# Four quads of gathered rows on chip instead of two, and attention's operands under the expert buffers

## The reference

```python
x = x + attention(layernorm(x))        # 16 heads of 128, causal; W_K, W_Q, W_V, W_O
x = x + ffn(layernorm(x))
# ffn: 32 experts, 8 of them for each token, besides a shared expert of width 256
topk_idx, topk_w = route(x)            # sigmoid scores, 4 of 8 groups kept, top 8, weights normed, times 2.5
coeff = zeros(T, E).at[arange(T)[:, None], topk_idx].add(topk_w)
for g, u, d, c in experts:             # gate, up, down: 256 to 128 and back
    out += c[:, None] * ((silu(x @ g.T) * (x @ u.T)) @ d.T)
out += silu(x @ shared_gate.T) * (x @ shared_up.T) @ shared_down.T
```

## Time and profile before

| | |
|---|---|
| median of 3 runs | 1460.2 us (1456.81 to 1460.44) |
| the profiled execution | 1459.2 us |
| its span | 1457.5 us |
| TensorE busy | 1327.4 us (91%), mean granted clock 0.973 |
| DVE busy | 961.8 us (66%) |
| ScalarE busy | 723.9 us (50%) |
| POOL busy | 610.6 us (42%) |
| DMA | 218.55 MB, mean 150 GB/s |

### The profile page before, as it was taken

How to read it: one execution, slowest core, us unless ns; L and a number is a source line. 1 busy time by engine, 2 the same in 40 slices (tenths; PEclk the granted TensorE clock), 3 DMA queues, 4 the chain that set the end, 5 groups by cost and what they waited for, 6 DMA issues and landing times.

```text
span 1457.5 us, 29253 instructions
## 1 busy us (share of the span) xinstructions
PE 1327.4 (91%) x8754; PEld 1167.5 (80%) x8754; DVE 961.8 (66%) x2024; ACT 723.9 (50%) x1664; POOL 610.6 (42%) x571
## 2 busy tenths in 40 slices
PE   5999999999999898998999999999888888789883
PEld 4888888888888786887778888888678878779883
DVE  5666667666678777687866766666686533356538
ACT  2555555555555444444455555555355545445441
POOL 4634536426342722303064553630005654445556
PEclk9999999999999899999999999999999999899997
DMA  3355443463452440000021111110459998999963
GB/s 121 113 170 180 135 139 130 151 209 112 139 170 70 166 153 15 19 12 26 5 66 37 65 39 55 43 61 30 142 198 382 341 363 260 362 387 326 334 186 90
DMA packets 120184, 218.55 MB, mean 150 GB/s; under 512 B 9504, under 2 KB 91424, under 8 KB 120096
## 3 DMA queue, kind: packets, MB, share of 16 engines
q1 hardware_dynamic: 56688, 132.58, 26.4%
q10 hardware_dynamic: 51120, 51.26, 10.5%
q0 software_dynamic: 12288, 33.57, 6.7%
HBM read 121.42 MB, written 95.94 MB: 149 GB/s over the span
## 4 chain that ended last, share of the span: by engine, by line
PE 63%; DVE 12%; DMA 11%; issue 6%; ACT 3%; POOL 2%; SPq 1%; another core or an unknown queue 1%; ACTq 0%; DVEq 0%; POOLq 0%
PE ps_t L795 6%; PE ps_s L735 6%; PE ps_s L737 6%; PE ps_s L736 6%; PE ps_x L735 5%; PE ps_x L736 5%; PE ps_x L737 5%; DMA xq<-xs 4%; PE ps_z L735 4%; PE ps_z L737 4%; PE ps_z L736 4%; DMA ring<-ws 4%; PE ps_t L735 3%; PE ps_t L737 2%; PE ps_t L736 2%
## 5 line engine op out<-in xcount | busy, mean ns | idle before, releaser
L1055 ACT ACTIVATE prob<-ps_s,neg_max 128x128 f32<-128x128 f32 (+7 forms) x256 | 189.6, 742 | 299.9 <-DVE neg_max L1236 289.2
L1251 DVE TENSOR_TENSOR pT_lo<-ps_t,pT_hi 128x512 fp32r<-128x512 f32 (+2 forms) x320 | 191.2, 601 | 66.0 <-ACT pT_hi L1071 57.9
L1236 DVE TENSOR_REDUCE neg_max<-ps_s 128x1 f32<-128x128 f32 (+7 forms) x256 | 188.7, 749 | 11.3 <-PE ps_s L786 9.8
L795 PE MATMUL ps_t<-ident,prob 128*128 128x128 f32 x1152 | 180.7, 275 | 15.4 <-DVE pT_lo L1251 9.4
L633 POOL DMA_INDIRECT xs<-xn,slots x128 | 127.0, 993 | 156.6 <-PE ps_z L737 108.2
L1071 ACT ACTIVATE pT_hi<-ps_t 128x512 fp32r<-128x512 f32 (+2 forms) x320 | 165.0, 534 | 50.9 <-PE ps_t L795 47.6
L795 PEld LDWEIGHTS ps_t<-ident,prob 128*128 128x128 f32 x1152 | 140.9, 141 | 49.8 <-DVE pT_lo L1251 15.6
L560 POOL TENSOR_TENSOR a_hi<-raw_a,zero 128x512 fp32r<-128x512 f32 x32 | 33.4, 1043 | 284.2 <-PE ps_x L737 258.3
L735 PE MATMUL ps_s<-k_hi,q_hi 128*128 128x512 f32 (+2 forms) x384 | 148.6, 387 | 0.7 <-DVE k_lo L1231 0.4
L736 PE MATMUL ps_s<-k_lo,q_hi 128*128 128x512 f32 (+2 forms) x384 | 133.5, 348 | 0.0
L737 PE MATMUL ps_s<-k_hi,q_lo 128*128 128x512 f32 (+2 forms) x384 | 133.4, 347 | 0.0
(11 more groups left out here) (288 smaller groups left out, 3882.6 us busy)
## 6 DMA issues: line engine op xcount, KB each, us to landing
ring<-ws SPq DMA_DIRECT2D x60, 768.0 KB
ws<-split_to SPq DMA_DIRECT2D x34, 768.0 KB, 4.1
xs<-taken SPq DMA_DIRECT2D x16, 1536.0 KB, 10.1
xq<-xs ACTq DMA_DIRECT2D x48, 512.0 KB
xs<-yq ACTq DMA_DIRECT2D x48, 512.0 KB
raw<-experts_dram SPq DMA_DIRECT2D x34, 384.0 KB, 4.6
raw_a<-w_a_dram SPq DMA_DIRECT2D x15, 512.0 KB, 10.4
raw_o<-w_o_dram SPq DMA_DIRECT2D x31, 128.0 KB
```

The costliest lines, as they stand in the source:

```text
L795: last = pe.transpose(bank[:, j * P:(j + 1) * P], prob[c][:, j, n * P:(n + 1) * P], ident[:, :])
L1055: act.activation(prob[c][:, j, 0:width(r)], ps_s[r % 2][:, 0:width(r)], ACT.Exp, bias=neg_max[:, r:r + 1], accum_out=row_sum[:, c, j:j + 1 ...
L1236: dve.tensor_reduce(neg_max[:, r:r + 1], ps_s[r % 2][:, 0:width(r)], AX.X, ALU.max, negate=True).then_inc(s_max, 1)
L1251: dve.tensor_tensor(lo, ps_t[m % 2][:, j * P:], hi.bitcast(F32), ALU.subtract).then_inc(s_bank_free, 1)
```

## The change

Four quads of rows are on chip instead of two (XQ). The first four are issued behind A(0), and quad q+4 when quad q is evicted. Batch 1's quads can be loaded only when its scatter is done; so its first quad (24) is issued where it was before, at the second task of quad 22, and its quads 25 and 26 with it; the two places before that issue nothing (rows_due). The memory comes from moving nine of attention's operands into the region that it releases. Ten gather buffers that lay in them are gone and eight new ones are added, so GATHERS is 62. The number of transfers, their sizes and all computation stay.

```diff
--- before.py
+++ after.py
@@ -100,7 +100,7 @@
-YQ, GATHERS = 4, 64
+YQ, XQ, GATHERS = 4, 4, 62
@@ -279,12 +279,7 @@
     raw_a, a_hi, a_lo = sb("raw_a", [P, 1024]), sb("a_hi", [P, 1024], F32R), sb("a_lo", [P, 1024], F32R)
-    raw_b, b_hi, b_lo = sb("raw_b", [P, 512]), sb("b_hi", [P, 512], F32R), sb("b_lo", [P, 512], F32R)
-    raw_o = sb("raw_o", [P, 2, D])
-    o_hi = [sb(f"o_hi{a}", [P, D], F32R) for a in range(2)]
-    o_lo = [sb(f"o_lo{a}", [P, D], F32R) for a in range(2)]
-    pL_hi, pL_lo = sb("pL_hi", [P, 2 * P], F32R), sb("pL_lo", [P, 2 * P], F32R)
-    z_hi, z_lo = sb("z_hi", [P, NQ], F32R), sb("z_lo", [P, NQ], F32R)
+    raw_b = sb("raw_b", [P, 512])
@@ -326,6 +321,12 @@
+        b_hi, b_lo = [sb(w, [P, 512], F32R, attention) for w in ("b_hi", "b_lo")]
+        raw_o = sb("raw_o", [P, 2, D], F32, attention)
+        o_hi = [sb(f"o_hi{a}", [P, D], F32R, attention) for a in range(2)]
+        o_lo = [sb(f"o_lo{a}", [P, D], F32R, attention) for a in range(2)]
+        pL_hi, pL_lo = [sb(w, [P, 2 * P], F32R, attention) for w in ("pL_hi", "pL_lo")]
+        z_hi, z_lo = [sb(w, [P, NQ], F32R, attention) for w in ("z_hi", "z_lo")]
@@ -340,14 +341,12 @@
-    yg = [sb(f"yg{n}", [P, D])[:, :] for n in range(16)]
+    yg = [sb(f"yg{n}", [P, D])[:, :] for n in range(24)]
...
-    yg += [t[:, n * D:(n + 1) * D].bitcast(F32) for t in (b_hi, b_lo) for n in range(2)]
-    yg += [t[:, :].bitcast(F32) for t in (*o_hi, *o_lo)] + [raw_o[:, a, :] for a in range(2)]
-    xq = [sb(f"xq{n}", [P, 4, D])[:, :, :] for n in range(2)]
+    xq = [sb(f"xq{n}", [P, 4, D])[:, :, :] for n in range(XQ)]
@@ -922,12 +921,12 @@
-                pe.wait_ge(s_xq[u // 2 % 2], 16 * (u // 4) + 16)
+                pe.wait_ge(s_xq[u // 2 % XQ], 16 * (u // 2 // XQ) + 16)
@@ -1079,8 +1078,15 @@
-            act.dma_start(xq[q % 2], xs[b][i * NQ:(i + 1) * NQ, :].rearrange("(t p) d -> p t d", p=P))\
-                .then_inc(s_xq[q % 2], 16)
+            act.dma_start(xq[q % XQ], xs[b][i * NQ:(i + 1) * NQ, :].rearrange("(t p) d -> p t d", p=P))\
+                .then_inc(s_xq[q % XQ], 16)
+
+        def rows_due(u):
+
+            q = u // 2 + XQ
+            if u % 2 == 0 or q >= B * PT // 2 or PT // 2 <= q < PT // 2 + XQ - 2:
+                return []
+            return range(PT // 2, q + 1) if q == PT // 2 + XQ - 2 else [q]
@@ -1099,7 +1105,7 @@
-                    for q in range(2):
+                    for q in range(XQ):
                         load_rows(q)
@@ -1119,8 +1125,8 @@
-                if u % 2 and u // 2 + 2 < B * PT // 2:
-                    load_rows(u // 2 + 2)
+                for q in rows_due(u):
+                    load_rows(q)
```

More of the change, by code:

```diff
@@ L396, in build @@
     s_ring, s_w = [sem(f"ring{n}") for n in range(RING)], sem("weights")
-    s_xq, s_xT, s_xs_hi, s_xs_lo = [sem(f"xq{n}") for n in range(2)], sem("xT"), sem("xs_hi"), sem("xs_lo")
+    s_xq, s_xT, s_xs_hi, s_xs_lo = [sem(f"xq{n}") for n in range(XQ)], sem("xT"), sem("xs_hi"), sem("xs_lo")
     s_gu, s_silu, s_h = sem("gu"), sem("silu"), sem("h")
@@ L929, in transpose_rows @@
                     last = pe.transpose(ps_xT[u % 2][:, at:at + P],
-                                        xq[u // 2 % 2][:, u % 2 * 2 + j, d * P:(d + 1) * P], ident[:, :])
+                                        xq[u // 2 % XQ][:, u % 2 * 2 + j, d * P:(d + 1) * P], ident[:, :])
             last.then_inc(s_xT, 1)
```

## The result

The changed kernel takes 1448.1 us (median of 6 runs, 1446.3 to 1451.0), the kernel before 1458.5 (6 runs, 1453.4 to 1463.2): a ratio of 0.9926, interval 0.9899 to 0.9954. It is 10.4 us faster. The profiled execution took 1448.1 us, its span is 1446.3, 11.2 us less than before.

The account below looks back on a forecast made before the run. TensorE, busy 91% of the span, was held in the expert part by late row loads while DMA engines were full. Terms 15 + 1 + 2 - 1 = 17 us gave 1443 us, range 1429 to 1458.

Parts of the forecast that it names:

- What bounds, and the lead: Expert part: row loads take 11.9 us against 8.3 us of lead; four quads give 19.4, removing 22.7 us of waits.
- Memory: Moved attention operands and 62 gather buffers instead of 64: no cost, at most 1 us for the last two gathers.
- More loads at once: Extra row loads at task 0 and before batch 1, 0.374 us per issue on ScalarE: cost 1 us, 0 to 1.5.
- Stretches up to 1240: Expert part before batch 1's weights: gains of 2 us (1130 to 1178) and 1 us (1178 to 1210, bound by weights).
- Stretch 1240 to 1385: Batch 1's full-DMA stretch: gain 15 us, from 3 to 21; limits 20.8 (TensorE) and 15.2 to 27 (DMA).
- the 7 us for the clock: 1240 to 1385: TensorE's granted clock of 0.90 and 0.91 loses at most 13.9 us; half taken as gain, 7 us.
- the 13.8 us of waits: 1240 to 1385: TensorE's waits for rows, 10.6 + 3.2 us, all taken as possible gain.
- DMA-bound throughout (1455): Rival, chance 0.25: every wait for rows becomes a wait for weights; only early bytes gain, 5.4 us less 1.
- Everything goes (1425): Rival, chance 0.10: the weight ring's lead absorbs all; 22.7 us of waits and some 12 us of half clock go.
- slower (1479): Rival, chance 0.06: the row backlog delays 36 weight loads; 1 us longer each costs 18 us, 2 us gives 1479.
- nothing (1460): Rival, chance 0.04: another wait, hT_lo at 12.9 us, takes up what the row wait leaves; no gain.
- The signs named: Profile after: no row waits over 0.5 us, more weight waits, DMA share over 1.02, batch 1's last task some 17 us earlier.

Follow-up runs that it names:

- e2: The changed kernel with three quads of rows on chip instead of four, 62 gather buffers; 0.9903 of the kernel before.
- e6: The kernel before (two quads), but weight loads after the first eight bring only half their block, output not the reference's; 0.9794 of the kernel before, 1431.0 us.
- e1: The changed kernel's memory plan and 62 gather buffers, but two quads of rows, issued where the kernel before issues them; 0.9995 of the kernel before.
- e11: The changed kernel itself (four quads), run again on the third chip; 0.9932 of the kernel before, median 1452.9 us.
- e9: The kernel before itself (two quads), run again and profiled on the third chip; 1.0013 of the kernel before, median 1462.1 us.
- e3: The changed kernel with four quads ahead in batch 0 and two in batch 1; 0.9951 of the kernel before, 7.1 us gained.
- e4: The changed kernel with two quads ahead in batch 0 and four from the start of batch 1; 0.9942 of the kernel before, 8.1 us gained.
- e7: The changed kernel (four quads), but weight loads after the first eight bring only half their block, output not the reference's; 0.9787 of the kernel before, 1428.7 us.

## Why the prediction was right, and where its sizes were off

The forecast was faster, 17 us to 1443; measured 10.4, to 1448.1, inside the range of 1429 to 1458. The mechanism was right. The size was not, and a range that reached from 2 us of gain to 31 hides that.

*What bounds, and the lead.* Right. Rows were late because a load needed 11.9 us where the order of the code gave 8.3; with five or seven tasks of lead the wait is gone (e2, after), and with half the bytes of weights it is down to 3.4 us at the old lead (e6).

*Memory: nothing.* Right (e1, 0.9995).

*More loads at once.* The step that was wrong in kind, though not the largest in time. I priced an issue at 0.374 us, from the kernel before, and took 1 us in all, 1.5 at most. With more row loads ahead the issue itself becomes slow: 13.7 us of added issue time on ScalarE's queue. Not all of it reaches TensorE; in the changed kernel's profile the waits for hT_lo that directly follow a slow issue are 1.6 and 1.0 us, against a rise of that line of 6.2. The path that I named (the issue, hT_hi, DVE, TensorE) was the right one.

*Stretches up to 1240.* Forecast 2 + 1 - 1 us, before the cost 3; measured 2.8 in the first comparison, right, but 5.1 in the third group (e11 against e9) and 7.7 in the first (e3 against e1). So the agreement is in part luck. That the chains of weights would turn every gain into a wait for weights did not hold fully in those; the cause of this difference is open.

*Stretch 1240 to 1385.* This is the term that was mis-sized: forecast 15 us, measured 7.7 for all of batch 1 (10.5 - 2.8), and 3.5 in the third group. In the first group it was 14.2 (e4 against e1). The two limits, TensorE's 20.8 us and the DMA engines' 15.2 or more, were set and nothing for what else TensorE would wait for. The stretches tell the two parts of the 20.8 apart. Of the 7 us for the clock some 5 came, by this estimate: 909 matmuls kept TensorE busy 122.2 us from 1240 to 1385 before (0.134 us each), 935 of them 120.4 us from 1235 to 1375 after (0.129 us each). Of the 13.8 us of waits only 3 came: TensorE's idle time in these stretches fell from 22.8 to 19.6 us. In batch 1 other waits took the place: for weights 4.0 to 8.2, for hT_lo 6.3 to 8.6, and "issue" 1.4 to 6.4. The rise for weights repeats (e9 to e11: 9.7 to 16.3 over both batches) and so does one for hT_lo (14.4 to 18.2), part of it behind slow issues. The rise of "issue" does not: the gate product's is 8.0 in e9 with two quads and 6.8 in e11 with four. That the other waits had lain under the wait for rows, because the engines rested in it, is my reading and was not tested by itself. The 13.8 us was also the number of one execution: batch 1 waits 7.7 us for rows in e9 and 20.5 in e1. I had seen hT_lo, at 12.9 us, and made of it a rival that takes everything, at 0.04, rather than a deduction from the forecast.

*DMA-bound throughout (1455).* In part: the chain of batch 1 now runs through ring<-ws, at 378 GB/s. But e6 and e7 show that DMA was not the only limit. The Trainium skill, DMA: Bandwidth & Descriptors, section "Issuing engines are not separate DMA queues", was the rule that spoke against the change. The DMA share agrees with it, 1.02 in the first 85 us of batch 1 before and after, and so do e6 and e7, at 327 and 325 GB/s; e1 to e4 show that an earlier issue pays all the same.

*Everything goes (1425), slower (1479), nothing (1460).* None occurred. Loads of weights take a little longer: those on the chains of the expert part took 6.2 to 7.7 us before, eight of them, and 6.7 to 8.9 after, nine of them, 7.1 and 7.7 on the mean. In the count of the slower rival 0.6 us each costs 11 us. What it cost can't be read off; TensorE's waits for weights rose by 6.5. (By the terms of that rival a load comes every (6.91 + 0.82) / 2 = 3.9 us, not 4.3; the issues themselves come every 4.2 us from 1092 to 1130 and every 4.5 from 1240 to 1320.)

*The signs named.* Waits for rows gone, weights up, clock of batch 1 up (0.94 and 1.00), batch 1's first task 2.8 us earlier, tail the same (44.8 and 44.1 us): as forecast. Not as forecast: the last expert task was to be 17 us earlier and task 104 is 10.5; the waits for weights rose more in batch 1 (4.2 us) than in batch 0 (2.3); the DMA share is 0.97 to 1.02, not over 1.02.

## What to carry to other kernels

The lead of a prefetch is to be counted in tasks from the issue to the use, not in buffers, and set against the landing time under the load of that stretch: five tasks did it here, and the sixth and seventh brought nothing. A deeper prefetch can have a price at its issue: look at the longest issue in the view of its line, not only at the median, and at what stands behind it on the engine that issues. When a wait is removed, others come in its place, so the forecast needs a deduction for each wait that already has a line of its own in the view, not only the limits of the two busiest resources. And the wait that is to be removed is worth reading in more than one execution. Where a stretch is bound by DMA, the next gain is in bytes or in another stretch: a few lines for the tail gave half as much again.

## What the runs showed of the hardware

An issue of a 512 KB load or store on ScalarE's queue takes 0.37 to 0.39 us in the median, and with two quads of rows ahead 1.1 us at most. With three or four it takes at times 1 to 4.5 us, most of these in the stretches with a DMA share near 1.0; with the weights halved it stays under 0.7 us. What the issue waits for is open.

A 512 KB load of rows lands in 3.8 us at the least and 12.5 at the most in e1 with two quads, and in 9.4 to 18.2 us in batch 1 of e4 with four.

The runs fall in two kinds. In the first group the kernel before takes 1437.9 us, in the others 1458 to 1463. The traces of the two kinds differ too, in how many updates of semaphores they hold (about 15000 and 11000) and in waits that have no named end: ScalarE's "remote" waits are 17 to 42 us in the one kind and none in the other. The missing updates can explain missing names, not times; what makes the 20 us is open, and no experiment here tells it apart. More quads were quicker than two on both kinds.
